# Four attention layers rewritten: scores with queries on the partitions, 32x32 block transpositions, and the value product on eight 32x64 tiles

## The reference, cut to what matters

```
a0  attention, 16 heads of 64, one key and value head for all (shared), no mask
    linear layer on values rounded to a 6-bit grid in blocks of 32
a1  causal attention, 16 heads of 64
    the same linear layer
a2  causal attention over a latent of 32 (shared keys and values)
m0  mixture of 8 experts (top 2) and a shared expert
a3  causal attention with biases
m1  the same mixture of experts
```

```
q, k, v = x Wq, x Wk, x Wv
s       = q k^T / 8               (1024 queries x 1024 keys; causal: keys up to the query)
p       = exp(s - max over keys) / sum over keys of the same exp
y      += (p v) Wo
```

## Time and profile before

| | |
|---|---|
| median of 3 runs (lowest, highest) | 3053.14 us (3047.66, 3053.48) |
| profiled execution, its span | 3052.27 us, 3050.4 us |
| busy PE / DVE / ACT / POOL | 2823.4 / 1749.3 / 1196.1 / 1479.3 us |
| matmul records | 16065 |
| attention a0, a1, a2, a3 | 811.7, 627.9, 580.4, 638.5 us |

### The profile page before, as it was taken

One profiled execution on the slowest core, in us unless ns is written; L12 is line 12 of the kernel. 1 busy time (PEld: TensorE's weight loads), 2 busy tenths in 40 slices (PEclk: granted clock), 3 DMA queues, 4 the chain that ended last, 5 costly groups with the idle time before them and its releaser, 6 DMA issues. The chain is left out here.

```text
span 3050.4 us, 41067 instructions
## 1 busy us (share of the span) xinstructions
PE 2823.4 (93%) x16065; PEld 1207.0 (40%) x16065; DVE 1749.3 (57%) x2337; ACT 1196.1 (39%) x1607; POOL 1479.3 (48%) x932
## 2 busy tenths in 40 slices
PE   4999999999949999999948999999787999999978
PEld 3333333333324444444423444444333444444433
DVE  2566666666573555555573666666543555555653
ACT  2344444444413444444412444444222444444422
POOL 1576677766703555555502555555301555555520
PEclk9999999999958999999956999999897999999979
DMA  4000000000000000000001000000000000000000
GB/s 101 1 1 1 1 1 1 1 1 1 1 1 16 1 1 1 1 1 1 1 0 28 1 1 1 1 1 1 1 0 1 1 1 1 1 1 1 1 1 14
DMA packets 21345, 14.63 MB, mean 5 GB/s; under 512 B 3233, under 2 KB 20001, under 8 KB 21026
## 3 DMA queue, kind: packets, MB, share of 16 engines
q1 hardware_dynamic: 21154, 12.01, 1.6%
HBM read 9.91 MB, written 2.10 MB: 4 GB/s over the span
## 5 line engine op out<-in xcount | busy, mean ns | idle before, releaser
L765 POOL TENSOR_TENSOR sums<-sums,p 128x1024 f32<-128x1024 f32 (+3 forms) x704 | 1352.0, 1920 | 696.6 <-PE ps L549 626.4
L680 DVE TENSOR_REDUCE half_max<-ps 128x2 f32<-128x1024 f32 (+3 forms) x640 | 703.4, 1099 | 665.0 <-PE ps L530 537.5
L609 ACT ACTIVATE p<-ps 128x1024 f32<-128x1024 f32 (+3 forms) x704 | 597.6, 849 | 666.8 <-PE ps L509 384.1
L506 PE MATMUL ps<-q,k 64*128 64x512 f32 (+3 forms) x3328 | 819.0, 569 | 0.0
L549 PE MATMUL ps<-p,v 128*64 128x512 f32 (+3 forms) x2816 | 635.0, 530 | 0.0
L509 PE MATMUL ps<-max_row,pick 64*128 64x512 f32 (+3 forms) x1664 | 572.2, 681 | 0.0
L700 DVE RECIPROCAL inverse<-total 128x128 f32<-128x128 f32 x512 | 478.8, 940 | 51.2 <-ACT total L650 40.8
L506 PEld LDWEIGHTS ps<-q,k 64*128 64x128 f32 x3328 | 251.3, 185 | 509.0 <-issue 340.4
L530 PE MATMUL ps<-k_near,q_near 64*128 64x512 f32 (+2 forms) x1664 | 340.7, 403 | 27.9 <-DVE half_max L680 21.4
L680 DVE TENSOR_REDUCE neg_max<-ps 128x2 f32<-128x256 f32 x192 | 158.5, 826 | 331.0 <-PE ps L535 330.7
L755 POOL CAST k_near<-k 128x512 fp32r<-128x512 f32 x72 | 44.0, 611 | 464.4 <-ACT k L634 261.7
(11 more groups left out here) (138 smaller groups left out, 2067.4 us busy)
## 6 DMA issues: line engine op xcount, KB each, us to landing
q_w<-in_wq SPq DMA_DIRECT2D x3, 512.0 KB
o_w<-in_wo SPq DMA_DIRECT2D x3, 512.0 KB
k_w<-in_wk SPq DMA_DIRECT2D x2, 512.0 KB
v_w<-in_wv SPq DMA_DIRECT2D x2, 512.0 KB
out<-x SPq DMA_DIRECT2D x4, 256.0 KB, 2.8
scratch<-in_wq_t SPq DMA_DIRECT2D x1, 512.0 KB, 5.1
scratch<-in_w_out SPq DMA_DIRECT2D x1, 512.0 KB, 7.2
wq_latent<-scratch SPq DMA_DIRECT2D x1, 512.0 KB, 3.3
```

The costliest lines, as they stand in the source:

```text
L506: nc.tensor.matmul(out[:, head, 0:width], a.k[rows, key_slot(i, 3), k * P:(k + 1) * P], a.q[rows, i % 3, s * BANK + lo:(s + 1) * BANK], st ...
L609: act.activation(probabilities(g)[:, :, lo:BANK], score[g % 2][:, :, 0:BANK - lo], ACT.Exp)\
L680: last = v.tensor_reduce(out, chunk_ps[:, :, 0:hi - lo], AX.X, ALU.max, negate=True)
L765: pool.tensor_tensor(sums, sums, probabilities(g)[:, :, lo:BANK], ALU.add).then_inc(summed, 1)
```

## The change

The attention phase is written anew; the others keep their computation.

- The scores are computed once, in float32, with 128 queries on the partitions and up to 512 keys in the free dimension (a chunk). Two PSUM buffers of two banks take turns. A *cycle* is one query tile of one item, 8 cycles an item, tiles 7 to 0; without a mask each has two chunks, in causal items the tiles 7 to 4 have two (512 and 512, 384, 256 or 128 keys) and 3 to 0 one (512, 384, 256, 128).
- VectorE takes the negated maximum per row and joins two parts (`join_max`). ScalarE takes the exponential one head at a time, with the maximum as bias, and writes the row sum through `accum_out`. VectorE inverts the sum (128x2) and GpSimd multiplies the probabilities by it, one head and chunk at a time.
- VectorE transposes the scaled probabilities in blocks of 32x32. So each group of 32 partitions holds 32 keys of every 128, with queries along the free dimension. The values are copied by 16 DMAs an item into all four groups of 32 partitions (`v4`).
- The product with the values is made of 32x64 tiles: 4 partition groups x 2 heads, 128 columns (4 query tiles x 32) each, summed over 32 blocks of keys (16 for the lower causal half). One unit of 4 query tiles is 256 matmuls. It is issued in shares behind the scores of later cycles: shares of a third without a mask, of 3, 3, 4 and 6 sixteenths, and one undivided, in causal items.
- Turned maxima, sums by ones, selection matrix, rounded copies, the reciprocals of 128x512 and GpSimd's additions are gone. The experts' weights share memory with the turned probabilities and are loaded in the norm phase ahead of each expert phase.

```diff
-LEAD = 10
-LAG = 2
-RING = 6
-QUARTERS = 4
+RING = 5
...
+        add(-1, ("q", 0, 0), ("k", 0, 1))
...
+            if causal:
+                if i >= 1:
+                    add_product(g + 1, unit(i - 1, 1), (1,))
+                    add(g + 2, ("out", i - 1, 0))
+                if i + 1 < ITEMS:
+                    if not shared:
+                        add(g + 2, ("v", i + 1, 1))
+                        add(g + 3, ("q", i + 1, 0), ("k", i + 1, 1))
...
+                if i < ITEMS:
+                    add_product(g + 5, unit(i, 0), (3, 3, 4, 6))
+            else:
+                if i >= 1:
+                    add_product(g + 1, unit(i - 1, 1), (1, 1, 1))
+                    add(g + 4, ("out", i - 1, 0))
+                if i + 1 < ITEMS:
+                    add(g + 4, ("q", i + 1, 1))
+                if i < ITEMS:
+                    add_product(g + 5, unit(i, 0), (1, 1, 1))
...
+            def score(c):
...
+                if c >= 2:
+                    pe.wait_ge(exped, c - 1)
...
+                for n in range(begin, end):
+                    k, c = some[n]
+                    skip = max(0, k - base) if causal else 0
+                    for row in range(4):
+                        rows = slice(32 * row, 32 * row + 32)
+                        for head, cols in enumerate(HEADS):
...
+                            last = nc.tensor.matmul(m.ps[cols, 4 + row, 32 * skip:P], values,
+                                                    turned_p(u)[rows, head, skip:UNIT, k * P + 32 * c:k * P + 32 * c + 32],
...
+            for g in range(FIRST, LAST):
+                if 0 <= g < CYCLES:
+                    for c in chunks_of[g]:
+                        score(c)
...
+            def exps(c):
+                g, part, lo, hi = chunks[c]
+                if part == 0:
+                    act.wait_ge(shift_ready, g + 1)
+                if c >= RING:
+                    act.wait_ge(turned, c - RING + 1)
...
+                for head in range(2):
+                    last = act.activation(a.p[:, c % RING, head, 0:hi - lo],
+                                          m.ps[:, 2 * (c % 2) + head, 0:hi - lo], ACT.Exp,
+                                          bias=shift[:, head:head + 1],
+                                          accum_out=a.sums[:, g % 4, part, head:head + 1])
+                last.then_inc(exped, 1)
...
+            for g in range(FIRST, LAST):
+                if 0 <= g < CYCLES:
+                    row_max(chunks_of[g][0])
+                if 0 <= g - 1 < CYCLES:
+                    invert(g - 1)
+                if 0 <= g < CYCLES and two_parts[g]:
+                    row_max(chunks_of[g][1])
+                    join_max(g)
+                if 0 <= g - 1 < CYCLES:
+                    for c in chunks_of[g - 1]:
+                        turn(c)
...
+            for g in range(CYCLES):
+                pool.wait_ge(inverted, g + 1)
+                for c in chunks_of[g]:
...
+                    for head in range(2):
+                        p = a.p[:, c % RING, head, 0:hi - lo]
+                        last = pool.tensor_scalar(p, p, a.inverse[:, g % 4, head:head + 1], 1.0, ALU.mult, ALU.mult)
+                    last.then_inc(scaled, 1)
```

More of the change, by code:

```diff
@@ L475, in attention_phase @@
-        ring_slot = [n - 1 for n in sums_done]
-        step_of_ring = [g for g in range(TOTAL) if step(g)[2] > 0]
-        def probabilities(g):
-            i, s, k, _ = step(g)
-            return a.sums[:, unit(i, s) % 2] if k == 0 else a.p[:, ring_slot[g] % RING]
+        ORDER = tuple(range(QT - 1, -1, -1))
+        UNIT = 4
+        CYCLES = ITEMS * QT
+        chunks, chunks_of = [], []
+        for g in range(CYCLES):
+            i, t = g // QT, ORDER[g % QT]
+            keys = (t + 1) * P if causal else S
+            parts = [(lo, min(lo + BANK, keys)) for lo in range(0, keys, BANK)]
+            chunks_of.append([len(chunks) + n for n in range(len(parts))])
+            chunks += [(g, n, lo, hi) for n, (lo, hi) in enumerate(parts)]
@@ new lines, in attention_phase, with add, add_product @@
+        extras = {}
+        def add(g, *ops):
+            extras.setdefault(g, []).extend(ops)
+        def add_product(g, u, shares):
+            some, done = blocks_of(u), 0
+            for n, share in enumerate(shares):
+                upto = len(some) * sum(shares[:n + 1]) // sum(shares)
+                add(g + n, ("product", u, done, upto))
+                done = upto
+        add(-1, ("q", 0, 0), ("k", 0, 1))
+        if shared:
+            add(0, ("v", 0, 0), ("k", 1, 1))
+        else:
+            add(0, ("v", 0, 0))
@@ L482, in attention_phase, with small_banks, slot, key_slot @@
+        def small_banks(region):
+            return m.ps[:, 4 + 2 * region:6 + 2 * region, :]
+        def slot(i):
+            return i % 2
+        def key_slot(i):
+            return i % B if shared else i % 2
+        def turned_p(u):
+            return a.turned[:, u % 2]
         block = ctx.enter_context(nc.Block())
@@ L540, in mix_step @@
-            def mix_step(g):
-                i, s, k, lo = step(g)
-                pe.wait_ge(exped, g + 1)
-                if k == 0:
-                    pe.wait_ge(mixed_out, unit(i, s))
-                if k == 0 and s == 0 and (not shared or i < B):
-                    pe.wait_ge(small_out, use_of["v", i, 0 if shared else 1] + 1)
-                end = g + 1 == end_step(i, s)
-                for head, rows in enumerate(HEADS):
-                    last = nc.tensor.matmul(mix[rows, lo:BANK], a.v[:, key_slot(i, 2), k, value_columns(head)],
-                                            probabilities(g)[:, head, lo:BANK], start=k == 0, stop=end,
-                                            skip_group_check=True)
-                last.then_inc(weighed, 1)
@@ L620, in take_small @@
                 act.wait_ge(small_mm, n + 1)
                 if kind in "qk":
[L622 to L625 removed]
+                    if i >= 2 and not (shared and kind == "k"):
+                        act.wait_ge(scored, unit_end(unit(i - 2, 1)))
```

496 lines of the change are left out of this document (203 added, 293 removed).

## The result

The changed kernel takes 3595.75 us (median of 4 runs, 3590.18 to 3599.36) where the kernel before takes 3050.40 on the same chip: ratio 1.179, 95% interval 1.176 to 1.181. The forecast was 2979, the range ended at 3240.

A forecast was written before the change was run, and what follows sets the result against it. TensorE's column count and changes of form were taken to bound the attention phases. 802 us without a mask plus 3 x 594 causal gave 2584, 75 less than 2658.5, hence 2979 us; range 2860 to 3240.

The forecast's parts named there:

- the one that adds projections to a cycle: Attention cycles holding projections: 0.6 us more, with output and q unmasked, with output and v in causal items.
- I cost no fall: TensorE's granted clock stays at 0.95 to 1.00; a fall to 1.2 GHz would add over 100 us a phase.
- I take 16 ns: TensorE's product with the values: 16 ns a record, so a third of a unit (171 records) takes 2.7 us.
- Rival 1: TensorE does not keep the product's pace, deciding from 19 ns a record; at 25 ns 3175 us; chance 0.20.
- The chain: Unmasked two-chunk cycle: exponentials, scores, maximum, sum and reciprocal, second maximum, joining one after another, 6.0 us.
- The row sum: ScalarE's row sum behind each exponential: 0.15 us per head; a tenth more each would add 64 us.
- Hidden, by 0.3 us: Unmasked cycles: VectorE's two transpositions and GpSimd's scaling fit beside exponentials and scores, 0.3 us to spare.
- rivals 2 and 3: GpSimd's scaling becomes the link, 3125 us, chance 0.12; a transposition takes two cycles a column, 3510 us, chance 0.06.
- Rival 2: GpSimd's scaling becomes the link from 0.75 us a piece; at 0.87, 3125 us; chance 0.12.
- Causal items: The three masked attention phases: 36.2 us an item from tile-to-tile intervals, 594 us a phase.
- some 80%: Sign: TensorE busy some 80% of the time, its idle time ended by ScalarE's exponentials.
- a2 is not the phase that loses: Refuting sign: a2 was forecast to lose 14 us while a1 and a3 gain 34 and 44.

The follow-up runs named there:

- experiment 8: The product of a unit left undivided in the phase without a mask, against the kernel with the two edits: 3449.80 us, ratio 1.132.
- experiment 1: Projections wait only for the emptying of their own pair of PSUM banks, against the changed kernel: 3238.25 us, ratio 1.061.
- experiment 14: VectorE transposes one of two heads from the third unit on, against the two edits plus unread TensorE products in score-only cycles: 3067.38 us, ratio 1.005.
- experiments 6: The exponential's shift is the first chunk's maximum alone, second maximum and joining left out, against the two edits: 3021.69 us, ratio 0.992.
- 12: The second transposition of a wide cycle comes one cycle later, against the kernel with the edits of 10: 2853.18 us, ratio 0.935.
- the two edits: Waits by own bank pair and the undivided causal share halved, a2's q on the other bank pair, against the changed kernel: 3119.40 us, ratio 1.024.
- the edits of 10: Four shares for the unmasked phase's first unit and unread TensorE products in a2, against the one-maximum kernel: 3025.95 us, ratio 0.991.
- experiment 4: Copies of the values into the four partition groups left out from the third item on, against the changed kernel: 3598.09 us, ratio 1.179.
- after: The changed kernel itself, against the kernel before: 3595.75 us, ratio 1.179.
- experiment 7: Product made for two of four partition groups, half of its matmuls left out, against the two edits: 3189.75 us, ratio 1.046.
- experiment 11: Unread TensorE products behind each share and in score-only cycles, against the half-product kernel of experiment 7: 3145.61 us, ratio 1.031.

## Why the prediction was wrong

The step that failed is the one that adds projections to a cycle: "0.6 more where output and q projections (four matmuls, 3.9 us) stand in that slot", and in causal items "5.2 + 0.6 for output and v projections". It counted their work and not the waits in front of them, nor what is queued behind: the scores of the next cycle. Measured, the slot of a0 costs 11.9 instead of 6.6 us, the two of a1 and a3 20.6 and 20.9 together instead of 10.4. Taking the wait away gave 357 of the 617 us between forecast and result, the clock that fell in it included; a smaller share for the undivided product gave 119 more.

- **Clock.** "I cost no fall" was wrong: 832 us at half speed. Alone, with the waits kept, preventing much of it gave 133 us; with the waits gone, 11. The clock is mostly a surcharge on the waits, and I had named its price but given it no part in the sum.
- **Pace and supply.** "I take 16 ns" held for a share (15.9), with some luck: it lies between an estimate by columns (14.5) and 17.5 from four bf16 matmuls of 64 columns, another kind of work. Here the Trainium skill's floor of about 25 ns between starts ("TensorE: Matmul & The Clock Gate", section "Wait — 56ns, not 53.3ns?") and this trace differ, and the trace decides. Rival 1 had the right worry, "120,000 instructions", but the wrong form: not a slower record but blocks of 256 instructions, of which a burst has one to two and a third in hand (127 to 297 records in experiment 8, 144 in the rows of a1 above). Where one share was 256 records, the cycle grew from the forecast 5.45 to 8.5; halving it gave 119 us on top of experiment 1.
- **The chain.** Its mechanism was right, 6.0 us forecast, 5.67 measured. The row sum was over-priced: the instruction is 202 ns but overlaps on both sides, so that a head follows the other after 0.67 us, where 0.75 was counted. "Hidden, by 0.3 us" is true of the transpositions (experiment 14), but the margin is nothing: two take 2.58 us, not 2.3, and the chain around them is shorter than forecast.
- **GpSimd and transposition** (rivals 2 and 3) cost 0.69 and 1.24 us, as taken. Rival 2 came true only once the second maximum was gone: experiments 6 and 12.
- **Causal items.** With the two edits an item is 37.7 to 38.9 us against 36.2 forecast, and a0 807 against 802. That a0 agrees so well is partly luck: undisturbed cycles are 0.3 us shorter than forecast, and the means of its cycles are 5.7 to 6.3 us (the 6.6 with the projections aside), with 44 us of pauses inside the product and 106 us at half speed in the phase. The four phases sum to 2726, 142 over the forecast's 2584; (2.5 + 1.5 + 2.7) x 16 = 107 of it are the causal items. In a1 the 2.5 us are spread: 0.5, 0.3, 0.9 (two cycles), 0.65, 0.3 and 0.3 over the forecast, the last cycle 0.55 under it. What causes them stays open.
- **Signs named.** TensorE was to be busy "some 80%": 76, 71, 72 and 71%. That "a2 is not the phase that loses" was named as a refutation: all lost. By us a0 lost least (73), then a2 (92), a3 and a1 (189 and 192); against its forecast a2 is the nearest (78 over), a0 83. The sign that maxima wait behind TensorE's product came true in a1, where a share was 256 records (the 8.5 us cycle); the sign that transpositions wait for GpSimd without a mask did not, with 1.5 us in all of a0.

## What to carry to other kernels

When an in-order engine serves a chain and odd jobs, write for each odd job what it waits for and what stands behind it in its queue; its own duration is the small part. A counter semaphore that means "all earlier ones are drained" makes every job wait for the slowest consumer: wait by buffer. Cut work of many tiny matmuls into short bursts with other work between: here halving bursts of 256 float32 records (512 instructions) gained, 512 records in one piece cost 330 us, and going from 160 to 176 records down to 128 in half of the product of a0 made no clear difference. And when an experiment frees one limit, look for what it had covered: the second maximum hid GpSimd's delay; its removal alone gave 98 us, with the later transposition (and the edits of 10, which changed nothing by themselves) 266.

## What the runs showed of the hardware

- TensorE's instructions come in blocks of 256; in a long burst of small matmuls one in 3.5 to 4.0 us (experiment 8), though the transfer of one lasts 1.06 us. A burst at 15.9 ns a record outruns that after 127 to 297 records. Taking other DMAs away (share 0.20 to 0.04 in a1) changed the kernel's time by nothing (experiment 4).
- Eight 32x64 float32 tiles side by side: 15.9 ns a record of 128 columns (after); four: 27.5 to 30 (experiment 7).
- Leaving out half of the product's matmuls made the kernel 70 us slower, nearly all of it in a2, where the granted clock was 0.71 against 0.89 (experiment 7). With other work on TensorE in their place, 44 of the 70 us came back (experiment 11). A high busy share beside a low clock is no sign of much work, as the low clock itself makes the busy time longer.
